# A decoder kernel on one core: keys and values of the second attention projected ahead, kept in DRAM, and biased by GpSimd

## What is computed

```python
x = x + _L0_attn_ref(_layernorm(x, axis=-1), ...)      # decaying attention
x = x + _L0_xattn_ref(_layernorm(x, axis=-1), ctx_1024, ctx_1024, mask, ...)
x = x + _L0_ffn_ref(_layernorm(x, axis=-1), ...)       # 8 experts, 2 per token
x = x + _L1_attn_ref(_layernorm(x, axis=-1), ...)      # time and channel mix
x = x + _L1_xattn_ref(_layernorm(x, axis=-1), ctx_1024, ctx_1024, fside_BxSxS2_0, ...)
x = x + _L1_ffn_ref(_layernorm(x, axis=-1), ...)

def _L1_xattn_ref(query, key, value, bias_struct, Wq, bq, Wk, bk, Wv, bv, Wo, bo, lambda_bias):
    Q = _split_heads(query @ Wq.T + bq)
    K = _split_heads(key @ Wk.T + bk)
    V = _split_heads(value @ Wv.T + bv)
    scores = jnp.einsum('bhqd,bhkd->bhqk', Q, K) * SCALE
    scores = scores + lambda_bias * bias_struct[:, None, :, :]
    attn = jax.nn.softmax(scores, axis=-1)
    out = jnp.einsum('bhqk,bhkd->bhqd', attn, V)
    return out.transpose(0, 2, 1, 3).reshape(...) @ Wo.T + bo
```

## Time and profile before

| | us |
|---|---|
| median of 3 runs | 1997.98 (1991.75 to 2000.43) |
| the profiled execution, its own time | 1993.02 |
| its span, first to last instruction | 1991.2 |
| first attention layer, from 0 to | 88 |
| causal attention | 88 to 416 |
| experts: token loop | 416 to 465 |
| experts: picks and lists, first gather | 465 to 508 |
| experts: 43 groups | 508 to 1030 |
| time and channel mix | 1030 to 1490 |
| second attention | 1490 to 1936 |
| last layer | 1936 to 1991 |

### The profile page before, as it was taken

One profiled execution on the slowest core, in us unless ns is written; L12 is line 12 of the kernel. 1 busy time (PEld: TensorE's weight loads), 2 busy tenths in 40 slices (PEclk: granted clock), 3 DMA queues, 4 the chain that ended last, 5 costly groups with the idle time before them and its releaser, 6 DMA issues. The chain is left out here.

```text
span 1991.2 us, 40593 instructions
## 1 busy us (share of the span) xinstructions
PE 1691.7 (85%) x13412; PEld 1393.7 (70%) x13412; DVE 1248.1 (63%) x4276; ACT 1103.6 (55%) x2520; POOL 566.1 (28%) x719
## 2 busy tenths in 40 slices
PE   6577777774899999999956999999988999999963
PEld 5455555553688888889944877787766888888842
DVE  6689999858211111111118999999936988888856
ACT  2299999920222222223325666666636888888845
POOL 3433233230211111101025566666520000000017
PEclk9899999976899999999977999999998999999975
DMA  3100010025455555558930000000001000000002
GB/s 117 47 26 25 19 26 18 2 80 183 135 180 187 181 186 183 185 174 267 323 129 14 19 22 22 22 22 22 12 12 40 23 23 23 23 23 23 2 1 85
DMA packets 102046, 154.64 MB, mean 78 GB/s; under 512 B 5760, under 2 KB 85504, under 8 KB 101088
## 3 DMA queue, kind: packets, MB, share of 16 engines
q1 hardware_dynamic: 85600, 125.25, 19.1%
q0 software_dynamic: 6480, 17.70, 3.0%
q10 hardware_dynamic: 9776, 9.31, 1.3%
HBM read 134.54 MB, written 17.69 MB: 76 GB/s over the span
## 5 line engine op out<-in xcount | busy, mean ns | idle before, releaser
L1836 ACT ACTIVATE moe_hT<-moe_p_h,lane_a 128x256 f32<-128x256 f32 (+1 forms) x344 | 131.4, 433 | 370.3 <-PE moe_p_h L1788 370.0
L1788 PE MATMUL moe_p_h<-moe_gT,moe_w 128*128 128x256 f32 (+1 forms) x1376 | 256.1, 345 | 0.8 <-issue 0.8
L1330 ACT ACTIVATE xb_pr<-xb_sc,xb_nmax 128x256 f32<-128x256 f32 x512 | 225.5, 502 | 50.7 <-DVE xb_nmax L1407 50.6
L1798 PE MATMUL moe_p_y<-moe_w,moe_hT 128*128 128x256 f32 x1136 | 252.3, 379 | 0.0
L1788 PEld LDWEIGHTS moe_p_h<-moe_gT,moe_w 128*128 128x128 f32 x1376 | 227.6, 192 | 25.7 <-issue 1.2
L1798 PEld LDWEIGHTS moe_p_y<-moe_w,moe_hT 128*128 128x128 f32 x1136 | 212.5, 190 | 27.1
L1407 DVE CUSTOM_DVE_ANT_0 xb_sc<-xb_p_s,xb_neg 128x256 f32<-128x256 f32 x512 | 187.0, 420 | 47.2 <-PE xb_p_s L1182 43.7
L837 ACT ACTIVATE xa_pr<-xa_sc,xa_nmax 128x256 f32<-128x256 f32 (+1 forms) x512 | 204.0, 453 | 17.6 <-DVE xa_nmax L917 17.2
L1705 POOL DMA_INDIRECT moe_gx<-moe_tokens,moe_source_i x71 | 67.4, 949 | 457.2 <-PE moe_p_t L1775 400.6
L1956 DVE COPY moe_gT<-moe_p_t 128x512 f32<-128x512 f32 (+1 forms) x43 | 25.7, 599 | 232.3 <-PE moe_p_t L1775 232.3
L1981 DVE TENSOR_TENSOR moe_gy<-moe_p_y,lane_a 128x256 f32<-128x256 f32 x71 | 27.5, 421 | 229.1 <-PE moe_p_y L1798 229.1
(11 more groups left out here) (331 smaller groups left out, 3454.3 us busy)
## 6 DMA issues: line engine op xcount, KB each, us to landing
moe_w<-in_L_ffn_w_dram SPq DMA_DIRECT2D x86, 1024.0 KB
moe_rows_out<-moe_gy ACTq DMA_DIRECT2D x28, 256.0 KB
X<-in_x_dram SPq DMA_DIRECT2D x4, 1024.0 KB, 10.9
xa_ctx<-in_ctx_turned_dram SPq DMA_DIRECT2D x16, 256.0 KB, 2.8
moe_tokens<-moe_XN_s SPq DMA_DIRECT2D x16, 256.0 KB, 2.1
xb_ctx<-in_ctx_turned_dram SPq DMA_DIRECT2D x16, 256.0 KB
xb_raw<-in_fside_BxSxS_dram SPq DMA_DIRECT2D x16, 256.0 KB
out_dram<-X SPq DMA_DIRECT2D x2, 1280.0 KB, 5.2
```

The lines of the kernel that those rows point to most:

```text
L1330: last = act.activation(pr[:, n % RB, e, :], sc[:, n % RB, e, :], ACT.Exp, bias=nmax[:, n % RB, e:e + 1], scale=-1.0)
L1788: last = pe.matmul(p_h[n % 3][:, k * width:(k + 1) * width], w1[:, r, ic, (2 * n + k) * P:(2 * n + k + 1) * P], gT[:, r % 2, ic, 0:width], ...
L1798: last = pe.matmul(p_y[:, t * D:(t + 1) * D], hT[:, hc, t * P:(t + 1) * P], w2[:, r, hc, :], start=(hc == 0), stop=(hc == HC - 1))
L1836: last = act.activation(hT[:, 2 * n + k, 0:width], p_h[n % 3][:, k * width:(k + 1) * width], ACT.Gelu, bias=b1[:, bass.ds(e * HC + 2 * n + ...
```

## The change

The key and value projections of all 16 batches move from the second attention to the experts' front part. A unit there is the keys or the values of one batch (two halves of two products each). Sixteen units stand in the token loop, one a turn, in place of the warm-up products; three follow before the counting products, seven after them, six after the first six list products. ScalarE copies each unit out of PSUM (`read_kv`), SP stores it to a DRAM tensor `kv_all`. Weights and contexts lie meanwhile in slots 3 and 2 of the expert weights' ring; therefore SP loads the weights of groups 2 and 3 only after all units are stored and the second gather has landed. In the second attention SP loads keys and values of the next batch from `kv_all`, and GpSimd adds the biases into k and v.

```diff
@@ biased_attention, SP
-                sp.dma_start(ctx[:, s, :, :], ins["ctx_turned"]...).then_inc(ctx_in[s], 16)
+                sp.dma_start(k_in[:, s, :, :]..., kv_all[bass.ds(2 * b, 1), :, :]...).then_inc(kv_in[s], 16)
+                sp.dma_start(v_in[:, s, :, :]..., kv_all[bass.ds(2 * b + 1, 1), :, :]...).then_inc(kv_in[s], 16)
@@ biased_attention, GpSimd
+            def finish_keys(n, h, s):
+                wait_alone(pool, s_["stood_p"], (kv_in[s], 32 * h + 32))
+                if since(n, 1):
+                    wait_alone(pool, s_["stood_p"], (s_["scored"], UNITS * (n - 1)))
+                for c in range(DC):
+                    last = pool.tensor_scalar(k[:, s, c, :], k_in[:, s, c, :], cols[:, 1, c:c + 1], None, ALU.add)
+                last.then_inc(s_["k_ready"], 1)
+            def finish_values(n, s):
+                if since(n, 1):
+                    wait_alone(pool, s_["stood_p"], (s_["pv"], UNITS * (n - 1)))
+                for t in range(TB):
+                    last = pool.tensor_tensor(v[:, s, t, :, 0:DH], v_in[:, s, t, :]..., rows[:, 0, :]..., ALU.add)
+                last.then_inc(s_["v_ready"], 1)
...
             for b, h, s in long_turns(pool, drain=2):
                 if since(b, 2):
                     add(b - 2)
+                if has_next(b):
+                    finish_keys(b + 1, h + s, 1 - s)
+                    finish_values(b + 1, 1 - s)
                 if has_next(b, 2):
                     root(b + 2)
@@ biased_attention, TensorE
-                    if g == 1 and has_next(b):
...
-                        project_keys(b + 1)
                     if g == 2 and has_next(b):
                         project_queries(b + 1)
-                    if g == 3 and has_next(b):
-                        if since(b, 1):
-                            pe.wait_ge(s_["o_ready"], TB * b)
-                        project_values(b + 1)
@@ biased_attention, VectorE: finish_keys, finish_values and their calls removed
@@ experts_ffn, SP
+            sp.dma_start(w_kv..., ins["pack_xb"][:, DC * D:3 * DC * D]).then_inc(s_["wkv_in"], 16)
+            for n in range(4):
+                load_context(n)
             sp.dma_start(sh.b[:, :], ins["pack_mix"]).then_inc(sh.sems["mix_in"], 16)
             for b, h, s in turns(sp):
+                if b >= 3:
+                    store_kv(b - 3)
+                if b >= 4 and b % 2 == 0:
+                    load_context(b // 2 + 2)
                 sp.wait_ge(s_["normed"], b + 1)
                 sp.dma_start(tokens...).then_inc(stored_x[s], 16)
...
+            for u in range(B - 3, 22):
+                store_kv(u)
+                if u % 2 and u // 2 + 4 < B:
+                    load_context(u // 2 + 4)
             sp.wait_ge(s_["owned"], 1)
             for j, r, i in groups(sp):
+                if isinstance(j, int) and j == 2:
+                    for u in range(22, 2 * B):
+                        store_kv(u)
...
+                    for n in range(4):
+                        sp.wait_ge(kept_kv[n], 16 * B // 2)
+                    sp.wait_ge(drawn[1], 32)
@@ experts_ffn, TensorE (keep_busy removed)
+            def project_context(u, halves=(0, 1)):
+                n, m = divmod(u, 2)
+                for k in halves:
+                    if k == 0:
...
+                        if u >= 2:
+                            pe.wait_ge(s_["kv_read"], u - 1)
...
-                keep_busy(2)
+                project_context(b, (0,))
                 if has_next(b):
                     gate_tokens(b + 1, 1 - s)
-                keep_busy(2)
+                project_context(b, (1,))
+            for u in range(B, B + 3):
+                project_context(u)
             pe.wait_ge(s_["both_ready"], 1)
...
+            for u in range(B + 3, B + 10):
+                project_context(u)
             for g in range(2 * NT // 8):
...
                 last.then_inc(s_["hot_read"], 1)
+                if B + 10 + g < 2 * B:
+                    project_context(B + 10 + g)
@@ experts_ffn, ScalarE: one a turn in the loop, 3 behind it, 13 behind the exponentials
+            def read_kv(u):
+                act.wait_ge(s_["kv_proj"], u + 1)
+                if u >= 4:
+                    act.wait_ge(kept_kv[u % 4], 16 * (u // 4))
+                act.activation(held[:, u % 4, :], p_kv[u % 2][:, :], ACT.Copy).then_inc(s_["kv_read"], 1)
```

112 lines of the change are left out of this document (58 added, 54 removed).

## The result

| | median of the runs | profiled execution | its span |
|---|---|---|---|
| before | 1994.6 us (14 runs) | 1993.0 us | 1991.2 us |
| after | 2004.2 us (14 runs) | 2006.6 us | 2004.5 us |

The ratio is 1.005, with a 95% interval of 1.0038 to 1.0063: 7.6 to 12.6 us slower. It is small, and the interval does not reach 1. The kernel does less work in its second attention, as intended, and pays more for it in the experts' front.

The account below looks back on a forecast made before the run. TensorE bounds the token loop; VectorE's copy bounds second-attention steps 1 and 3. Front costs 13.6 + 1.1, second attention gives 9.9: +4.8 us on 1998.0, forecast 2003 us, range 1990 to 2017 (the forecast's own 1997 to 2008).

Parts of the forecast that it names:

- The steps of the second attention: Second attention: step 1 from 5.71 to 5.64 us, step 3 from 6.75 to 6.34; 1.1 and 5.7 us off.
- The busy share of 388 of 401 us, which spoke for 60 us: Rival for the second attention: TensorE's removed time is fully given back, 60 us, so 1950 us; chance 0.08.
- The start, -3.1 us: Start of the second attention: batch 0's values, 3.25 us at the low clock, no longer precede the first scores; 3.1 us off.
- some 0.7 us, which the wait for the queries absorbs: Second attention, batch 0: raw bias arrives behind one more load, some 0.7 us, hidden by the queries' wait; zero cost.
- GpSimd, nothing: Second attention: GpSimd's four bias additions, about 0.65 us each, 2.6 us a batch, add no time.
- The third rival: Second attention: GpSimd holds VectorE up in the bound chain, 1.3 us a batch, 19 us, 2022 us; chance 0.05.
- The first token store, +5 us: Token loop: first store queued behind 1536 KB more, landing 8 us after issue; third normalisation and TensorE wait 5 us.
- The turns: Token loop: 5.63 us a turn at the low clock, 3.0 at the high, with 5.1 us at the low clock.
- List steps, 0: Between loop and expert groups: six units fit beside list products 2.58 us apart at the high clock; no cost.
- list products over 2.6 us apart: Sign for the lists ahead of the first expert group: list products over 2.6 us apart would make the forecast wrong.
- The first rival: Experts' front: clock low 13.5 us, or low again in lists; 2007 to 2008 us, both 2012; chance 0.35.
- Its other half: Lists: TensorE's rest before the first list product lowers the clock; six steps of 3.9 instead of 2.58 us, 5 us.

Follow-up runs that it names:

- the two runs of the back alone: back_alone and back_vector: before's front with the change's second attention, projections left out; ratios 0.9954 and 0.9950.
- values_gap: Kernel before with only the values projected ahead, all 16 units behind the token loop, GpSimd adding their bias; 1988.7 us, ratio 0.9978.
- values_warm: values_drawn plus one more unread round of products behind the second attention's first scores; 1986.6 us, ratio 0.9956.
- values_drawn: values_gap with the second expert group's weights issued only when the gathers of the first two groups have landed; 1984.7 us, ratio 0.9956.
- front_alone: The change with before's second attention, which projects its own keys and values again; 2015.1 us, ratio 1.0115.
- the four kernels with this order: The change itself, front_alone, list_stores and start, all with the change's order of loads ahead of the first token store; ratios 1.005, 1.0115, 1.0054, 1.0027.
- late_loads: The change with contexts 1 to 3 behind the first three token stores and mixing weights behind the second group's weights; 2002.4 us, ratio 1.0050.
- back_alone: Before's front with the change's second attention, loading untouched context in place of kept keys and values, no projections; 1984.8 us, ratio 0.9954.
- back_vector: back_alone with VectorE instead of GpSimd adding the biases, in steps 1 and 3; 1981.2 us, ratio 0.9950.
- its three siblings: front_alone, list_stores and start, which share the change's token loop and load order; ratios 1.0115, 1.0054 and 1.0027.
- list_stores: The change with units 22 to 27 stored ahead of the first expert group's weights, 28 to 31 ahead of the second's; 2004.9 us, ratio 1.0054.
- start: The change with the second attention's side input loaded first and two unread rounds of products ahead of its first transposes; 1999.6 us, ratio 1.0027.

## Why the prediction was right, and where it was not

The forecast was 2003 us, the median 2004.2. That is closer than the sum deserves, and part of it is luck: the forecast started from a median of 1998.0, and before stands at 1994.6 in the longer series; what was added was 4.8 us, what the ratio shows is 7.6 to 12.6. Slower, but within 0.5%, was the likeliest case; the ratio of 1.005 lies on that line, and the sign and the range held. The sum was 14.7 us for the front, -3.1 for the start and -6.8 for the steps; the two profiled executions show 20.8, +0.4 and -7.6, in sum 13.6. By its own steps:

- **The steps of the second attention: right to the hundredth.** 5.64 and 6.34 forecast, 5.64 and 6.33 measured; batches of 25.02 us where 25.0 was said; 6.8 us forecast from first to last, 7.6 in after, 6.7 and 7.4 in the two runs of the back alone. Reading the step without the projection off batch 15 carried this. The busy share of 388 of 401 us, which spoke for 60 us, was no guide.
- **The start, -3.1 us: wrong in sum, right in its term.** The values' products are worth 3.1 us there, as values_gap shows (13.28 instead of 16.40). The step that failed was to count only them. The queries ran 3.78 us instead of 1.99; and a third load stood ahead of the side input, "some 0.7 us, which the wait for the queries absorbs", which in fact VectorE waits for in front of its statistics. Transposes 1.4 us later (9.17 instead of 7.76 us in), they and their copy 0.5 longer, the queries 1.8 longer: 3.7, less 3.3 for the values, is the +0.4 measured. I had named the load and let a wait absorb it that stands behind it, not beside it. Of the 1.4 us, 1.9 are the load and 0.3 the normalisation beside GpSimd, less 0.8 for the wait on the keys' bias that is gone. That the queries' low clock comes from the keys' removal is not shown: in the five executions with keys ahead of them they took 1.99 us twice (before, values_gap), and 3.12, 3.66 and 3.78 (values_warm, values_drawn, front_alone). Without keys or filler they were never below 3.67.
- **GpSimd, nothing: right in the steps.** Its operations took longer than the 0.65 us that I scaled from the 128x512 addition. Groups of the second attention in after:

```profile
L1120 POOL TENSOR_SCALAR xb_k<-xb_k_in,lane_a 128x256 f32<-128x256 f32 x28 | 26.0, 941 | 0.5 <-PE xb_p_s L1202 0.5
L1128 POOL TENSOR_TENSOR xb_v<-xb_v_in,lane_a 128x256 f32<-128x256 f32 x28 | 19.8, 729 | 65.8 <-PE xb_p_o L1232 65.8
```

  That is 3.3 us a batch instead of 2.6, on an engine that has 25. By the rule of the Trainium skill that I had weighed (SBUF — State Buffer, Who interferes with whom), VectorE's chain, whose shifts and copies read PSUM and at most one SBUF input, is not locked out; the trace agrees: of 63 steps all but four differ by 0.02 us at most between back_alone and back_vector. The third rival, 19 us, is out. Outside that chain VectorE was held up, by 0.3 us ahead of the first transposes.
- **The first token store, +5 us: right in kind, under in size.** It was +4.3 to +6.4 in the four kernels with this order (norm 2 at 10.97 to 13.05 instead of 6.67), and late_loads shows the cause by taking it away. The landing, forecast 8 us after issue, was 9.8.
- **The turns: right, but not the only limit.** 6.03 us at the low clock and 3.06 at the high, where I had 5.63 and 3.0; 6.8 us at the low clock where I had 5.1. The step that failed says of ScalarE's evictions that they "and the waits of SP for them cost nothing at 3.0 us a turn". SP's wait for the copy of a unit holds back the token store that follows it in the program, by 0.1 to 5.6 us in thirteen turns of after; beside kept units and contexts the stores' median landing went from 2.1 to 3.3 us as well, and VectorE waited for them seven times. In all, the totals were copied 20.1 us later in after and 15.8 to 17.8 in its three siblings; forecast 14.7. The whole front, to the source rows, came to 15.6 to 22.4 against 14.7. The first list product came 20.15 us later in after, where the signs said about 15.
- **List steps, 0: right for TensorE, wrong for the queue.** Each unit fits into 2.58 us beside its list product, as list_stores shows. What did not fit was the store of the unit: "ScalarE's evictions ... cost nothing" looked at the time of the copy and not at what the copy waits for. It stood 11.3 us and cost 2.2 in the lists (20.98 instead of 18.76; 0.5 and 1.6 in front_alone and start, which have the same code there). By one of the prediction's own signs, list products over 2.6 us apart, this part of it was wrong: 7.3 us lay between two of them, and 2.9 three times.

The first rival's price (over 2007) was not reached by the median, and its mechanism, a clock low for 13.5 us, did not occur in after: the clock was low for 6.8 us. The 13.5 us were themselves one draw: in the same loop of six executions the clock rose 6 to 14 us after the first warm-up product. Its other half, a low clock in the lists, occurred in part, with the gaps of 2.9 us. The excess in the loop came from SP's program and its queue.

What stays open: why the first token store held norm 2 until 10.97 in one execution and 13.05 in another with the same front, why the clock rises at such different moments in the same loop, and why the queries of the second attention ran at the low clock in some executions of a code and at the high one in others.
